# A four-layer hybrid kernel on one Trainium2 core: the output sum of the selective scan follows one turn behind the scan instead of two

## What is computed

```
def step(h, inp):
    d_t, x_t, B_t, C_t = inp
    dA = jnp.exp(d_t[..., None] * As)
    h = dA * h + (d_t * x_t)[..., None] * B_t[:, :, None, :]
    y = jnp.einsum('bkdn,bkn->bkd', h, C_t)
    return (h, y)
...
y = out_y[:, 0] + inv_y[:, 0] + wh_y + invwh_y
```

## Time and profile before

| | us |
|---|---|
| median of 3 runs | 791.63 |
| lowest and highest of them | 789.14, 793.08 |
| the profiled execution | 789.41 |
| its span, first to last instruction | 787.6 |

### The profile page before, as it was taken

The page is one execution under the profiler, slowest core; times in us unless marked ns, Lnnn a source line. Parts: engine busy times, 40 slices in busy tenths (PEclk is TensorE's granted clock), DMA queues, the critical chain, the costliest instruction groups (busy, mean ns, idle before and its releaser), DMA issues.

```text
span 787.6 us, 7064 instructions
## 1 busy us (share of the span) xinstructions
PE 701.5 (89%) x2462; PEld 352.8 (45%) x2462; DVE 605.5 (77%) x594; ACT 350.5 (45%) x387; POOL 413.6 (53%) x229
## 2 busy tenths in 40 slices
PE   5979999989999899998988767787798889999997
PEld 4633333333333233332332222355345577777775
DVE  5599999999999999999999949756794453334432
ACT  4676484556655744556544326133103243333331
POOL 4056998998999999999899910000061000000000
PEclk9979999999999999999999989999999999999999
DMA  5144564665554646545465442110640000000000
GB/s 169 35 160 140 187 213 159 213 229 168 198 175 161 236 158 207 195 141 197 166 237 191 157 185 113 45 71 1 256 171 1 0 1 1 1 1 0 0 0 27
DMA packets 30126, 97.76 MB, mean 124 GB/s; under 512 B 4132, under 2 KB 4870, under 8 KB 29358
## 3 DMA queue, kind: packets, MB, share of 16 engines
q1 hardware_dynamic: 30096, 97.38, 35.5%
HBM read 95.78 MB, written 1.59 MB: 124 GB/s over the span
## 4 chain that ended last, share of the span: by engine, by line
PE 41%; DVE 29%; issue 12%; POOL 9%; ACT 5%; DMA 3%; DVEq 0%; SPq 0%; POOLq 0%; ACTq 0%
PE ps L1733 15%; DVE area L1166 10%; POOL area L611 6%; PE ps L1468 6%; PE ps L1445 5%; DVE ps L1154 5%; PE ps L1749 4%; DVE area L354 3%; DVE area L1162 2%; DMA area<-c_rows 2%; PE ps L1436 1%; DVE small L426 1%; PE ps L1389 1%; POOL area L627 1%; DMA area<-in_w_dt_dram 1%
## 5 line engine op out<-in xcount | busy, mean ns | idle before, releaser
L611 POOL TENSOR_TENSOR area<-area 128x1024 f32<-128x1024 f32 x127 | 297.6, 2365 | 32.3 <-DVE area L1166 24.4
L1468 PE MATMUL ps<-area,cst 128*128 128x512 f32 x512 | 252.9, 621 | 5.9 <-POOL area L611 5.3
L1166 DVE TENSOR_TENSOR_SCAN area<-area,ps 128x1024 f32<-128x1024 f32 x111 | 249.8, 2274 | 4.1 <-ACT area L803 0.9
L803 ACT ACTIVATE area<-area,floors,par_sb 128x1024 f32<-128x1024 f32 x111 | 132.8, 1233 | 62.1 <-DVE area L1166 55.6
L1468 PEld LDWEIGHTS ps<-area,cst 128*128 128x128 f32 x512 | 89.3, 191 | 117.6 <-issue 95.6
L1154 DVE TENSOR_TENSOR ps<-ps,area 128x1024 f32<-128x1024 f32 x111 | 132.9, 1213 | 4.0 <-PE ps L1436 3.4
L1733 PE MATMUL ps<-stack,sel 128*128 128x512 f32 (+1 forms) x576 | 114.7, 359 | 0.7 <-DVE sel L1351 0.7
L1733 PEld LDWEIGHTS ps<-stack,sel 128*128 128x128 f32 x576 | 95.8, 189 | 19.4 <-issue 1.2
L458 DVE COPY area<-ps 64x1024 f32<-64x1024 f32 x32 | 39.3, 1227 | 72.1 <-PE ps L1749 41.4
L456 ACT ACTIVATE area<-ps 64x1024 f32<-64x1024 f32 x32 | 32.6, 1020 | 94.2 <-PE ps L1733 51.3
L708 POOL COPY area<-area 128x256 f32 (+1 forms) x16 | 6.4, 403 | 129.8 <-PE ps L1749 129.8
(11 more groups left out here) (300 smaller groups left out, 695.5 us busy)
## 6 DMA issues: line engine op xcount, KB each, us to landing
area<-c_rows SPq DMA_DIRECT2D x145, 512.0 KB, 4.4
area<-phi_scaled SPq DMA_DIRECT2D x1, 4104.0 KB, 24.3
area<-in_m_phi_dram SPq DMA_DIRECT2D x4, 1024.0 KB, 7.9
area<-phi_scaled SPq DMA_DIRECT2D x1, 4096.0 KB, 13.9
area<-in_q_t_dram SPq DMA_DIRECT2D x1, 1024.0 KB, 13.5
c_rows<-tok SPq DMA_DIRECT2D x28, 32.0 KB, 2.8
area<-in_dft_dram SPq DMA_DIRECT2D x1, 784.0 KB
area<-in_m_u_dram SPq DMA_DIRECT2D x1, 768.0 KB, 5.9
```

What stands on the lines that cost most here:

```text
L611: pool.tensor_tensor(scan_order(prod[:, u % PRODS, :], k), lines(state[:, u % STATES, :], k), lines(c_sb[:, u % COPIES, :], k), MUL).then_ ...
L803: act.activation(dst, delta[:, n % 2, :], ACT.Exp, bias=floors[:, k, i:i + 1], scale=par_sb[:, k, i:i + 1]).then_inc(sig("decayed"), 1)
L1166: dve.tensor_tensor_scan(state[:, u % STATES, :], decay[:, u % DECAYS, :], drive_pair(u), 0.0, MUL, ADD).then_inc(sig("scanned"), 1)
L1468: mm = pe.matmul(ps[:, 6 + h, :], con("center"), half(prod[:, u % PRODS, :], h), start=(u % (UNITS // 2) == 0), stop=(u % (UNITS // 2) == ...
```

## The change

One number in the planner of PE's order:

```diff
@@ -129,7 +129,7 @@
 
         AREA = 36 * L - 640
         DECAYS, STATES, PRODS, COPIES = 3, 4, 3, 3
-        LAG = 2
+        LAG = 1
         area = sb("area", [P, AREA])
         cut = [0]
 
```

## The result

| | before | after |
|---|---|---|
| median of four runs, us | 792.36 (789.14 to 796.04) | 809.62 (803.57 to 810.78) |
| profiled execution, us | 789.41 | 808.47 |
| its span, us | 787.6 | 806.6 |
| first scan to the end of the last sum, us | 419.3 | 433.9 |
| the rest of the span behind that, us | 328.6 | 334.0 |

The kernel is slower by a ratio of 1.0197, with a 95% interval of 1.0166 to 1.0228: 17.3 us by the medians, where the prediction said 10 and its range ended at 807.5. I call "the stage" the stretch from the start of unit 0's scan to the end of unit 127's sum. It grew by 14.6 us. The layers behind it, which the change doesn't touch, took 5.4 us more in this execution, and what lies ahead of the stage 1.0 us less (39.7 and 38.7), which makes the 19.0 us between the spans.

What follows compares the result with a forecast made beforehand. DVE was taken to bound the stage by little, with PE nearly full. The terms 1.2 + 2.2 + 0.7 + 4.85 + 1.5 - 0.7 = 9.75, say 10 us, on 791.63 gave 801.5 us; range 794.5 to 807.5.

Steps and rivals of the forecast that it cites:

- The bound and the mechanism: In the stage, DVE bounds by little; PE, in order, waits for late products, delaying the next spreads and DVE.
- D: Behind the soft jobs of blocks 1, 2, 3 and 5, PE waits for products: 0.8 + 3 x 1.35 = 4.85 us.
- half of it is swallowed: Rival: products gain on PE's slots after the first loss, so 1.35 us is paid once, not four times; 796.5 us, chance 0.18.
- B: First soft job: the sum of unit 6 waits for its product, making unit 11's spread late; 2.2 us more.
- C: Skip term in image 0: its four records now stand ahead of unit 14's spread; 0.7 us.
- E: Small places later in a block, such as unit 35's spread and the second image's skip term; 1.5 us in all.
- F: End of the stage: POOL's buffer waits go, -1.0 us, and unit 126's late spread gives 0.3 back; -0.7 us.
- signs that the prediction named: POOL's L1468 waits nearly nothing; unit 11's scan about 3.4 us later; block 1's end wait about 1.6; last scan some 10 later.
- A: Start of the stage: unit 0's sum now stands ahead of unit 5's spread, making everything behind late; 1.2 us.
- rival on TensorE's clock: Longer PE waits bring one more spell at the lower clock in the stage, 4 us on top; 806 us, chance 0.10.
- worst case: By the skill's rule, a lower-clock spell in each of six blocks of the stage, some 24 us in all.
- Not slower: Rival: POOL, freed from buffer waits, runs far enough ahead that no sum waits; 790.6 us, chance 0.10.

Runs made afterwards that it cites:

- pair with half products: Two kernels, lag two as before and lag one as changed, both with POOL's products over half the columns; medians 791.01 us (ratio 0.9972) and 793.46 us (1.0010).
- last-block kernel: The kernel before with a lag of one in the last block only; median 791.88 us, ratio 0.9983.
- filled kernel: The changed kernel plus zero-weight matmuls on PE ahead of the product waits at units 6, 19, 31, 51, 99 and 121; median 802.05 us, ratio 1.0125.
- middle kernel: The kernel before with a lag of one only from the slot of unit 20 to the end of block 6; median 799.67 us, ratio 1.0086.
- kernel with one place filled: The changed kernel plus two zero-weight matmuls ahead of the wait for product 6 only; median 804.32 us, ratio 1.0142.

## Why the prediction was right in its mechanism and short in its size

**The bound and the mechanism** held. PE's list is in order, a sum stands for its product, the spreads behind it are late, and DVE with them. The pair with half products shows it: halve the product's length and most of the cost goes.

**D** was right in size and place: 0.88, 1.36, 1.42 and 1.37 us against 0.8 and three times 1.35. The forecast that DVE would read about 1.6 us of wait at the end of block 1 (0.42 + 1.19) came out too. The rival "half of it is swallowed" fell with it: all four places are paid, in every kernel with a lag of one there.

**B** was right for a clock of 1.00: 2.2 predicted, 2.20 and 2.29 with fillers. In after it was 3.64. **C** was 0.53 instead of 0.7. **E** was 2.1 instead of 1.5 with fillers, and 4.2 to 5.1 without. **F** was -0.93 for -0.7 with fillers, -0.3 without. For F alone the last-block kernel gave -1.5. The filled kernel, which has all of the predicted mechanism and hardly any of the clock's, came to 9.6 us of stage and 802.05 us in the median, against 9.75 and 801.5. That the sum came so close is in part luck: A fell 0.55 us short of its term in this profile and E was 0.63 over. Of the signs that the prediction named, POOL's waits for L1468 went, but the scan of unit 11 stood 4.3 us later instead of 3.4 and the last scan 17.2 us later instead of 10, and both overshoots are mostly the clock's: the filled kernel has 2.9 and 11.5.

**A** is not settled by its size. The changed kernels gave 0.62 to 1.54 us for the predicted 1.2, but the middle kernel lost 1.03 us at the same scans without any change there. The start lies in a spell at the lower clock in every kernel, and where its end falls shifts these scans by about as much as the term.

**The step that failed** is the rival on TensorE's clock. The sum has no term for it. The prediction gave it 0.10, as one more spell for 4 us, with the words "the clock of 1.00 with 3 us of standing speaks against it happening often". That row of before was of a stretch in which PE stood for short times, and it was one execution. The change makes more single stands of 1.9 to 2.9 us. The trace of before had such stands too, of 1.87, 1.92 and 2.49 us, with no spell behind them; only a second execution of the same kernel showed spells behind the last two. In both profiles of the changed kernel the clock fell at the first soft job and at the end of the stage, some 48 us after the first, and once more at unit 35 or 55, each time within 1.4 us of such a stand or in it (1.86 to 2.85 us in after). The excess of after over the filled kernel is 1.4 us at B, 2.9 in E and 0.6 in F, 5.0 in all, and nothing at C and D. Some 0.5 us of it, at unit 35, is the wait for the C row, so about 4.5 us are the clock's. In the second profile B, E and F exceed the filled kernel's by 4.4 us, and the start (A) by 0.9. So what came was that rival's case, the forecast's 9.75 us and some 4.5 on top. The prediction had priced it rightly, at 4, though for one spell where four came, and had given it a chance of 0.10. With the clock's 4.5 us the sum would have been 14.2, for stages that grew by 14.6 and 14.8. The first median lies 2.1 us above the end of the range even so, and the second, 805.17, lies inside it. What carried the first beyond the range is not shown; in its profiled execution the layers behind the stage took 5.4 us more. Between the two medians of the changed kernel (809.62 and 805.17) lies 807.4, 15.1 us above before's 792.3, where the stages say 14.6 and 14.8.

The sentence by the Trainium skill, in TensorE: Matmul & The Clock Gate (HAM oscillation), that a matmul stream which waits between its bursts falls back to half rate again and again, was nearer than my weighting of it. The traces agree that it recurs, four spells of after with 17.0 us in all, but not that it does so at every wait: PE waited 26 times for a product in that stage. Its worst case, 24 us, did not come: the spells cost about 4.5 us.

"Not slower" fell as its own argument said. POOL is freed of the buffers in after, but the product behind the soft job follows the soft product, and all four places D are paid.

**What stays open.** The layers behind the stage took 334.0 and 328.3 us in the two profiled executions of the changed kernel, 328.6 and 328.3 in those of before, and 328.4 to 332.7 in the others. They have spells at the lower clock of their own, and no edit here sets their number. For the executions that were not profiled the record has the time and the granted clock. Over the eight of the changed kernel the two go together: 803.57 us at 0.976, 804.54 to 804.69 at 0.974 and 0.972, 805.64 and 809.65 at 0.969, and 808.47 to 810.78 at 0.967 to 0.963. So the difference between the two medians, 809.62 and 805.17, goes along with how long the clock was low. Where in the unprofiled executions it was low is not known. Nor is it shown why one stand brings a spell and another of the same length, or the same stand in another execution, doesn't. Every spell inside the stage of every profile here, behind the one at the start, begins in a stand of PE or within 1.6 us of the end of one; these stands were of 1.4 us or more, but once of 0.93 and 0.62. Stands of up to 2.49 us passed without a spell. The first stand's spell can be taken away by fillers. Whether the one some 48 us later hangs on the first is only suggested by the kernel with one place filled.

## What to carry to other kernels

On an engine that works through its list in order, compare, for each consumer that is moved up, the time at which its input is ready with the time of its new slot. A deficit that follows a common start (here the end of `soft`) was paid at each of the four such places, and neither shrank nor was swallowed. A wait of 2 to 3 us on TensorE may be paid twice, as the wait and again as a sum at 1.2 GHz behind it, so price both, above all where the bound engine already stands for that sum. One profile of the kernel before is not enough to judge this by: here it showed one such spell late in the stage, and a second profile of the same kernel three. If the bound engine stands for TensorE now and then, thin TensorE's list in the slot ahead of it: that gave 0.5% here, where the shorter lag cost 2%.

## What the runs showed of the hardware

Spells at 1.2 GHz came in lengths of 3.4 and 6.8 us in the stage of most of the profiled executions, before's too, and their places shifted between executions of one kernel: 68.0, 115.8, 156.8 and 453.7 us in one, 70.9, 118.6, 224.4 and 456.6 in the other. Each was in or shortly behind a stand of PE, and stands of 2.21 and 2.49 us passed without one. A sum of four records that lay mostly in a spell took 3.38 to 3.78 us instead of 1.98. Matmuls with zero weights that add into an open sum kept the clock at 1.00 for 398 us on end, where the changed kernel without them had three spells in that stretch, in each of two profiles. Two matmuls more ahead of the wait for product 6 cost nothing, as the sum had to wait 1.02 us longer than they took (1.90 us).
